# The one-token shift ahead of the FFN: two SBUF transfers in place of two matrix products, with the statistics later on VectorE

## The chip, the cores and the metric

The kernel runs on one core of a Trainium2 chip. The metric is device time in microseconds (us): the median of several executions. A profiled execution gives the trace that is read here, with its own span from the first to the last instruction.

The engines are TensorE (PE for its products, PEld for its weight loads), VectorE (DVE), ScalarE (ACT), GpSimd (POOL) and SyncE (SP). SP issues the transfers here. Each engine works through its own list in order, and engines wait for one another on semaphores.

## What is computed

A relative-position attention layer runs first, then six layers of local attention and a gated FFN. All of it is float32, over 4 sequences of 512 tokens of width 128. What matters for the change is the token shift: in each layer the second half of the features is taken from the token before.

```python
def shift_tokens(t):
    a, s = jnp.split(t, 2, -1)
    s = jnp.pad(s, ((0, 0), (1, 0), (0, 0)))[:, :-1]
    return jnp.concatenate([a, s], -1)

def ffn_layer(x, g, bln, W1, b1, W2, b2):
    mu = x.mean(-1, keepdims=True)
    var = ((x - mu) ** 2).mean(-1, keepdims=True)
    xn = (x - mu) / jnp.sqrt(var + 1e-05) * g + bln
    hg = xn @ W1 + b1
    a, gate = jnp.split(hg, 2, -1)
    return a * jax.nn.gelu(gate, approximate=False) @ W2 + b2

for i in range(DEPTH):
    x = attn_layer(shift_tokens(x), Wqkv[i], q_scale[i], k_scale[i], Wo[i]) + x
    x = ffn_layer(shift_tokens(x), ln_g[i], ln_b[i], W1[i], b1[i], W2[i], b2[i]) + x
```

## The kernel before

The six layers are `local_layers`. A tile is 128 tokens on the 128 partitions. A sequence is a group of SEQT = 4 tiles, a layer has 4 groups, and all six layers make NT = 96 tiles in GROUPS = 24 groups. The running activations stay in SBUF, in `x` (128 partitions, 16 tiles, 128 features).

Every engine runs one loop over periods n, one tile a period, and each function called in it names the tile it works on: `project("K", n)`, `turn_qk(0, n - 1)`, `attend(n - 3, 0)`. So the order on each engine is the order in which the loop's body is written. With step = n % 4 and g = n // 4, the FFN's work of a group is put at fixed steps. These are the places that matter:

- **PE, step 3** (`shift`, lines 545 to 554): between the two halves of `attend(n - 3)`, two products with the constant matrix `down` write the shifted half of the features of group g - 1 into the PSUM bank `XS`. The first moves rows 0 to 126 of each tile down by one, the second brings row 127 of a tile to row 0 of the next. Later in the same period come `turn_p` (line 510), `turn_xn` (line 561: transposes of the normalised tiles) and `project_out` (line 541).
- **DVE, step 3** (`statistics`, line 701): right after `rotate(1, n)` (line 643) DVE waits for the shift and takes mean and variance of the four tiles, from the own half in `x` and the shifted half in PSUM. Then come `sum_probs` (674), `invert`, `sum_squares` of q and of k (652), `offsets` (713) and `divide` (687), which `turn_p` of the same period waits for.
- **POOL, step 0 of the next group** (`deviations`, lines 281 and 283): the reciprocal deviation from the variances. It stands ahead of `norms` (from line 248) and `scale` (line 275) of the next tile, which end in the q that `turn_qk` (line 473) transposes on PE.
- **ACT, step 0 of the next group** (`normalise`, line 393): eight activations that make `xn` from `x` and the shifted half. PE's `turn_xn` waits for them.
- **SP** (`windows`, lines 180 to 189): for each tile t, 16 transfers of 64 KB that copy v into `vwin`, 32 partitions at a time. They wait for `v_copied` of tile t and, because `vwin` has two buffers, for `o_summed`: `attend(t - 2)` must be done. Weights of the next layer are loaded by SP at n % 16 == 10.

In the period 4g + 3 PE runs `attend(4g)`. Its end is what SP's `windows(4g + 2)` waits for.

Of the kernel before, what the change touches and what calls it, by code (L numbers as in the profile page):

```python
# [8 lines left out]
P = 128  # L9
# [23 lines left out]
MASKED = -1e30  # L33
FIRST_BITS = float(0x5f3759df)
NEWTON = 3
TABLES = 2 + 2 * 2 * WT + 5

def at_least(eng, sem, count):

    if count > 0:
        eng.wait_ge(sem, count)

def local_layers(nc, x1, x, out_tiles, w, kept):
# [7 lines left out]
    with ExitStack() as ctx:  # L53
        def sb(name, shape, dt=F32):
            return ctx.enter_context(nc.sbuf_tensor(name, shape, dt))
# [9 lines left out]
        b2 = sb("b2", [P, 2, D])  # L65
        qkscale = sb("qkscale", [P, 2, 2, DH])
        ropes = sb("ropes", [P, 2, 2, SEQT * 2, DH])
        ident, identb, bias, down, rope = (kept[n] for n in ("ident", "identb", "bias", "down", "rope"))

        first_stats = sb("first_stats", [P, TILES, 6])  # L70
        first_meanvar = sb("first_meanvar", [P, TILES, 2])
# [21 lines left out]
        meanvar = sb("meanvar", [P, SEQT, 2])  # L93
        rstd = sb("rstd", [P, SEQT])
        offset = sb("offset", [P, SEQT])
        xn = sb("xn", [P, SEQT, D])
        xnT = sb("xnT", [P, SEQ])
        gelu = sb("gelu", [FW, 2, SEQ])
# [9 lines left out]
                 "k_made k_squared k_rotated k_added k_summed k_roped k_turned kT_copied clamped newtoned rnorm_made "  # L108
                 "v_made v_copied scored maxed scores_taken exped p_turned p_copied p_summed rinv_made p_normed o_summed "
                 "oT_copied y_made y_added stats_made b2_added var_made var_eps rstd_made ropes_made "  # L110
                 "offset_made xn_made xn_turned xnT_copied shifted h_made gelu_made h_ready f_made x_done finished stored").split()
        s = {n: ctx.enter_context(nc.semaphore("l_" + n)) for n in names}
        placed, tail = (s["placed0"], s["placed1"]), (s["tail0"], s["tail1"])
        PLACED, TAIL, LOADS = 14 * 16, 2 * 16, 6 * 16
        CLEARED = 3

        ROOM = {"K": 0, "QT": 1, "XT": 4, "H0": 2, "H1": 1, "H2": 0, "O": 2, "XS": 3, "F": 3, "KT": 1, "V": 0, "S": 2, "Q": 1, "PT": 0, "XN": 3, "Y": 4}
        FREED = {"Q": ("q_squared",), "K": ("k_squared",), "V": ("v_copied",), "QT": ("qT_copied",),
                 "KT": ("kT_copied",), "S": ("scores_taken",), "PT": ("p_copied",), "O": ("oT_copied",),  # L120
                 "H": ("gelu_made", "h_ready"), "XT": ("xT_copied",), "XN": ("xnT_copied",), "XS": ("xn_made",), "Y": ("y_added",),
                 "F": ("x_done",)}

        ONE = ("XT", "XN", "XS", "Y", "F")

        def room(kind, c=0):
            return ROOM[kind + str(c)] if kind == "H" else ROOM[kind]
# [1 line left out]
        def bank(kind):  # L129

            r = room(kind)
            return ring[:, r, 0, :] if r < 3 else (tpose, yps)[r - 3][:, :]
# [11 lines left out]
        def halves_of(g, tile):  # L144

            half = D // 2
            return x[:, g % BATCH * SEQT + tile, 0:half], bank("XS")[:, tile * half:(tile + 1) * half]

        def live(t):
            return 0 <= t < NT  # L150
# [1 line left out]
        def lives(g):  # L152
            return 0 <= g < GROUPS
# [10 lines left out]
        @block.sync  # L164
        def _(sp):
            def load_layer(layer):
                p = layer % 2
                at_least(sp, s["x_done"], BATCH * (layer - 1))
                sp.dma_start(qkscale[:, p, :, :], w["qk"][layer]).then_inc(s["scales_in"], 16)
                sp.dma_start(wqkv[:, p, :], w["wqkv"][layer]).then_inc(s["qkv_in"], 16)  # L170
                loads = [(w1[:, p, :], w["w1"][layer]), (w2[:, p, :, :], w["w2"][layer]),
                         (b1[:, p, :], w["b1"][layer]), (ln[:, p, :], w["ln"][layer]), (b2[:, p, :], w["b2"][layer]),
                         (wo[:, p, :, :], w["wo"][layer])]
                for dst, src in loads:
                    sp.dma_start(dst, src).then_inc(s["weights"], 16)

            def windows(t):
                if live(t):
                    p = t % 2
                    sp.wait_ge(s["v_copied"], t + 1)  # L180
                    at_least(sp, s["o_summed"], t - 1)
                    for r in range(2):
                        sp.dma_start(vwin[W2 * r:W2 * r + W, p, 0, :], v[P - W:P, (t + 2) % 3, r, :]).then_inc(tail[p], 16)
                    for win in range(WT):
                        for r in range(2):
                            rows = v[W * win:W * win + W, t % 3, r, :]
                            sp.dma_start(vwin[W2 * r + W:W2 * r + W2, p, win, :], rows).then_inc(placed[p], 16)
                            if win + 1 < WT:
                                sp.dma_start(vwin[W2 * r:W2 * r + W, p, win + 1, :], rows).then_inc(placed[p], 16)

            load_layer(0)
            sp.wait_ge(s["cleared"], CLEARED)
            for n in range(NT):
                windows(n)
                if n % (SEQT * BATCH) == 10 and n // (SEQT * BATCH) + 1 < DEPTH:
                    load_layer(n // (SEQT * BATCH) + 1)
            for b in range(BATCH):
                sp.wait_ge(s["finished"], b + 1)
                tiles = slice(b * SEQT, (b + 1) * SEQT)
                sp.dma_start(out_tiles[:, tiles, :], x[:, tiles, :]).then_inc(s["stored"], 16)  # L200
            sp.wait_ge(s["stored"], 16 * BATCH)

        @block.gpsimd
        def _(pool):
            nc.gpsimd.memset(v[:, 2, :, :], 0.0).then_inc(s["cleared"], 1)
            nc.gpsimd.memset(kT[:, :, 0:W], 0.0).then_inc(s["cleared"], 1)
            nc.gpsimd.memset(power[:, :], -0.5).then_inc(s["ready"], 1)
            nc.gpsimd.memset(eps[:, :], EPS).then_inc(s["ready"], 1)
            pool.wait_ge(s["ready"], 2)
# [221 lines left out]
        def _(pe):  # L431
# [110 lines left out]
                                                stop=j == PAIRS - 1)  # L542
                    last.then_inc(s["y_made"], 1)

            def shift(g):

                if lives(g):
                    pe.wait_ge(s["y_added"], SEQT * (g + 1))
                    at, half = g % BATCH * SEQT, D // 2
                    out = take("XS", g)[:, 0:SEQT * half].rearrange("p (t d) -> p t d", d=half)  # L550
                    nc.tensor.matmul(out[:, :, :], down[:, 0, :], x[:, at:at + SEQT, half:D], start=True, stop=False,  # L551
                                     skip_group_check=True)
                    nc.tensor.matmul(out[:, 1:SEQT, :], down[:, 1, :], x[:, at:at + SEQT - 1, half:D], start=False, stop=True,
                                     skip_group_check=True).then_inc(s["shifted"], 1)

            def turn_xn(g):
                if lives(g):
                    pe.wait_ge(s["xn_made"], g + 1)
# [47 lines left out]
            for n in PERIODS:  # L606
                step, g = n % SEQT, n // SEQT
                project("K", n)
                turn_qk(0, n - 1)
                turn_x(n + 2)  # L610
                if step == 0:
                    hidden(g - 2, 0)
                    hidden(g - 2, 1)
                    hidden(g - 2, 2)
                attend(n - 3, 0)
                if step == 3:
                    shift(g - 1)
                if step == 1:
                    project_ffn(g - 2)
                turn_qk(1, n - 1)  # L620
                attend(n - 3, 1)
                project("V", n)
                scores(n - 1, 0)
                project("Q", n + 1)
                scores(n - 1, 1)
                turn_p(n - 2)
                if step == 3:
                    turn_xn(g - 1)
                project_out(n - 3)

        @block.vector
        def _(dve):
# [62 lines left out]

            def statistics(g):
                if lives(g):
                    dve.wait_ge(s["shifted"], g + 1)
                    for tile in range(SEQT):
                        for n, half in enumerate(halves_of(g, tile)):  # L700
                            nc.vector.bn_stats(stats[:, tile, n, :], half).then_inc(s["stats_made"], 1)  # L701
# [63 lines left out]
            for n in PERIODS:  # L765
# [5 lines left out]
                take_scores(n - 2)  # L771
                add_y(n - 4)
                rotate(1, n)
                if step == 3:
                    statistics(g - 1)
                sum_probs(n - 2)
                invert(n - 2)
                sum_squares(0, n)
                if step == 0:
                    gate(g - 2, 0)  # L780
                    gate(g - 2, 1)
                    gate(g - 2, 2)
# [6 lines left out]
            dve.wait_ge(s["x_done"], GROUPS)  # L789

def layer_tables(nc, pool, ident, identb, bias, down, made):

    nc.gpsimd.memset(down[:, :, :], 0.0).then_inc(made, 1)
    nc.gpsimd.memset(bias[:, :, :, :], 0.0).then_inc(made, 1)
    done = 2
    for first in range(2):
        for win in range(WT):
            view = bias[W * win:W * win + W, first, :, :]
# [10 lines left out]
        pool.wait_ge(made, done + r + 1)  # L810
    nc.gpsimd.tensor_copy(identb[:, :], ident[:, :]).then_inc(made, 1)

    nc.gpsimd.tensor_copy(down[:, 0, 1:P], ident[:, 0:P - 1]).then_inc(made, 1)
    nc.gpsimd.tensor_copy(down[:, 1, 0:1], ident[:, P - 1:P]).then_inc(made, 1)

def layer_norm_tiles(nc, src, dst, name):
# [33 lines left out]
def relative_attention(nc, x_in, x1, attn, w, scratch, kept, rope):  # L851
# [9 lines left out]
    with ExitStack() as ctx:  # L861
# [19 lines left out]
        with ExitStack() as second:  # L881
# [76 lines left out]
            with nc.Block() as block:  # L958
# [202 lines left out]
                def _(pool):  # L1161
# [1 line left out]
                    pool.wait_ge(s["filled"], 1)  # L1163
                    nc.gpsimd.memset(vaug[:, :, :, DP:DP + 1], 1.0).then_inc(s["cleared"], 1)
                    pool.wait_ge(loaded, LOADS)
                    layer_tables(nc, pool, ident, kept["identb"], kept["bias"], kept["down"], kept["made"])
                    for c in range(ROUNDS):
                        for k in range(2):
                            pool.wait_ge(s["c_taken"], 2 * c + k + 1)
# [53 lines left out]
def whole_kernel(nc, x_in, out, attention, layers):  # L1223
    with ExitStack() as ctx:
        def sb(name, shape, dt=F32):
# [4 lines left out]
        x_tiles = x_in.rearrange("b s d -> (b s) d").rearrange(tiled, p=P)  # L1230

        x = sb("x", [P, TILES, D])
        kept = {"ident": sb("ident", [P, P]), "identb": sb("identb", [P, P], BF16), "down": sb("down", [P, 2, P]),
                "bias": sb("bias", [P, 2, PAIRS, W2], BF16), "rope": sb("rope", [P, 2, SEQT * 2, DH]),
                "wo": sb("wo_a", [P, D]), "bo": sb("bo", [P, D])}
        for n in ("made", "rope_loaded", "x1_loaded", "x1_biased"):
# [94 lines left out]
```

## Time and profile before

| | before |
|---|---|
| median of 3 runs | 2145.36 us (2140.11 to 2148.38) |
| span of the profiled execution | 2143.9 us |
| PE busy | 2022.6 us (94%) |
| DVE busy | 1497.0 us (70%) |
| ACT busy | 1286.6 us (60%) |
| POOL busy | 1522.5 us (71%) |

The page lists the busy time of each engine, the granted TensorE clock in slices of the span, the chain of work that ended last, the costliest groups of instructions by line, and the transfers. The trace can also be asked for one engine's instructions in order of time. In that view a row starts with the start time and the duration in us, and a note in brackets tells how long the engine had sat idle and what ended that. A duration of "x2" is from the start of the first to the end of the second. For SP a row is the issue of transfers, marked SPq, and not the time the data moves. The layers run from about 485 us to the end.

### The profile page before, as it was taken

What the parts mean: (1) busy time and instruction counts of PE and PEld (TensorE: products, weight loads), DVE (VectorE), ACT (ScalarE), POOL (GpSimd) and SP (SyncE); (2) the same over time, 40 slices, a digit from 0 to 9 for tenths busy, and PEclk for the clock granted to TensorE, in tenths of its full rate; (3) what the DMA queues carried; (4) which work ended last, traced back from release to release, by engine and by line L of the source; (5) the groups of instructions that cost most, each with busy time, mean ns of one, the idle gap of its engine ahead of it and who ended that gap; (6) DMA issues with size and microseconds to landing.
All of it is one profiled execution on the core that took longest, in us unless ns stands there. A gap on an engine that the chain in (4) does not pass through costs nothing.

```text
span 2143.9 us, 84229 instructions
## 1 busy us (share of the span) xinstructions
PE 2022.6 (94%) x35763; PEld 1356.1 (63%) x35763; DVE 1497.0 (70%) x2268; ACT 1286.6 (60%) x1844; POOL 1522.5 (71%) x2307
## 2 busy tenths in 40 slices
PE   4789999878999999999999999999999999999997
PEld 1455555545666667666766667666676666766675
DVE  2445454458877887777877787777877788778773
ACT  3567777634656665665656565566656666566653
POOL 3344444458878887788877778778887788777880
PEclk8899999998999999999999999999999999999998
DMA  4999999932323222242222422224222242222221
GB/s 125 289 347 355 344 357 344 348 126 61 74 62 111 68 65 65 63 113 67 72 62 62 113 62 69 65 62 120 63 66 62 63 117 70 62 62 63 68 72 43
DMA packets 120004, 261.51 MB, mean 122 GB/s; under 512 B 29092, under 2 KB 34128, under 8 KB 118864
## 3 DMA queue, kind: packets, MB, share of 16 engines
q1 hardware_dynamic: 119632, 256.13, 41.4%
q8 instruction: 285, 4.67, 1.0%
q14 instruction: 87, 0.71, 0.1%
HBM read 87.06 MB, written 68.29 MB: 72 GB/s over the span
## 4 chain that ended last, share of the span: by engine, by line
PE 68%; POOL 4%; DVE 3%; issue 2%; ACT 1%; POOLq 0%; DVEq 0%; ACTq 0%
PE ring L463 22%; PE ring L529 9%; PE ring L473 8%; PE yps L541 7%; PE ring L499 7%; PE ring L569 5%; PE ring L510 4%; PE tpose L579 3%; PE ring L491 1%; POOL roped L275 1%; DVE turned L643 1%; PE tpose L551 1%; DVE ss L652 1%; DVE stats L701 0%; POOL ss L248 0%
## 5 line engine op out<-in xcount | busy, mean ns | idle before, releaser
L643 DVE TENSOR_TENSOR turned<-ring,ropes 128x1024 f32<-128x1024 f32 x384 | 452.0, 1219 | 303.0 <-PE ring L463 303.0
L240 POOL TENSOR_TENSOR roped<-turned 128x512 f32<-128x512 f32 x384 | 522.5, 1386 | 170.4 <-PE ring L473 169.0
L463 PE MATMUL ring<-wqkv,xT 128*128 128x512 f32 x1152 | 567.4, 616 | 5.2 <-ACT xT L328 4.0
L275 POOL TENSOR_TENSOR roped<-roped,rnorm 128x1024 f32<-128x1024 f32 x192 | 361.5, 1904 | 7.5
L1170 POOL TENSOR_SCALAR less<-less,lowest 128x512 f32<-128x512 f32 x256 | 175.3, 697 | 240.0 <-DVE lowest L1139 240.0
L1139 DVE CUSTOM_DVE_ANT_0 less<-ps_b,shifted 128x512 f32<-128x512 f32 x256 | 166.6, 688 | 226.0 <-PE ps_b L1002 79.7
L463 PEld LDWEIGHTS ring<-wqkv,xT 128*128 128x128 f32 x1152 | 198.2, 192 | 161.0 <-issue 149.8
L369 ACT COPY pT<-ring 128x1024 f32<-128x1024 f32 x96 | 97.2, 1012 | 305.8 <-PE ring L510 305.8
L529 PEld LDWEIGHTS ring<-pT,vwin 64*64 64x64 f32 x12288 | 198.5, 134 | 51.9 <-issue 51.5
L317 ACT ACTIVATE squares<-ring 128x1024 f32<-128x1024 f32 x192 | 197.3, 1028 | 55.8 <-DVE turned L643 55.8
L529 PE MATMUL ring<-pT,vwin 64*64 64x32 f32 x12288 | 219.7, 220 | 4.9 <-issue 3.4
L652 DVE TENSOR_REDUCE ss<-squares 128x16 f32<-128x1024 f32 x192 | 221.3, 1184 | 1.2 <-ACT squares L317 0.9
L473 PEld LDWEIGHTS ring<-ident,roped 128*128 128x128 f32 x1536 | 174.5, 142 | 70.0 <-issue 38.4
L473 PE MATMUL ring<-ident,roped 128*128 128x128 f32 x1536 | 204.4, 276 | 8.7 <-ACT qT L335 2.9
L499 PEld LDWEIGHTS ring<-kT,qT 64*32 64x32 f32 x12288 | 139.5, 105 | 100.8 <-issue 99.2
L1002 PE MATMUL ps_b<-posm,qvT 32*128 32x512 f32 x512 | 149.1, 666 | 52.3 <-DVE lowest L1139 43.6
L541 PE MATMUL yps<-wo,oT 128*128 128x128 f32 x1536 | 188.3, 276 | 1.2 <-ACT oT L376 1.1
L541 PEld LDWEIGHTS yps<-wo,oT 128*128 128x128 f32 x1536 | 180.0, 193 | 1.6 <-ACT oT L376 1.6
L499 PE MATMUL ring<-kT,qT 64*32 64x64 f32 x12288 | 173.0, 224 | 4.9 <-issue 4.9
L1068 PEld LDWEIGHTS ps_b<-ident,less 128*128 128x128 f32 x1024 | 111.5, 142 | 94.3 <-POOL less L1170 79.2
L344 ACT COPY kT<-ring 128x1024 f32<-128x1024 f32 x96 | 97.0, 1011 | 100.6 <-PE ring L473 100.6
L1213 ACT ACTIVATE pT_a<-ps_b 128x512 f32<-128x512 f32 x256 | 141.3, 613 | 25.3 <-PE ps_b L1068 25.2
(133 smaller groups left out, 3234.7 us busy)
## 6 DMA issues: line engine op xcount, KB each, us to landing
vwin<-v SPq DMA_DIRECT2D x1536, 64.0 KB, 2.0
shifted<-scratch_w SPq DMA_DIRECT2D x64, 1024.0 KB, 12.6
scratch_w<-wrows SPq DMA_DIRECT2D x48, 1026.0 KB, 10.9
scratch_w<-x SPq DMA_DIRECT2D x16, 1026.0 KB, 10.4
wqkv<-in_l_wqkv SPq DMA_DIRECT2D x6, 1536.0 KB, 6.9
wo<-in_l_wo SPq DMA_DIRECT2D x6, 512.0 KB
w<-in_l_w SPq DMA_DIRECT2D x6, 342.0 KB
w<-in_l_w SPq DMA_DIRECT2D x6, 171.0 KB
```

Of the source, the lines that this page charges most:

```text
L240: nc.gpsimd.tensor_tensor(halves[2][:, :, side, :], halves[0][:, :, side, :], halves[1][:, :, 1 - side, :], ALU.add).then_inc(s[name + "_a ...
L275: nc.gpsimd.tensor_tensor(whole, whole, norm, ALU.mult).then_inc(s[name + "_roped"], 1)
L317: nc.scalar.activation(squares[:, n, :], ring[:, room(name.upper()), :, :].rearrange("p b c -> p (b c)"), ACT.Square).then_inc(s[name + "_ ...
L463: last = nc.tensor.matmul(out[:, half, :], xT[:, t % SEQT * P:(t % SEQT + 1) * P], wqkv[:, layer_of(t), at + half * 512:at + (half + 1) * ...
L473: last = nc.tensor.transpose(out[:, j * P:(j + 1) * P], roped[:, n, j * P:(j + 1) * P], ident[:, :])
L499: last = nc.tensor.matmul(out[W * win:W * win + W, r, j * W2:(j + 1) * W2], qT[rows, j, W * win:W * win + W], kT[rows, j, at:at + W2], sta ...
L529: last = nc.tensor.matmul(out[a * DH:(a + 1) * DH, r, at:at + W], vwin[rows, p, win, j * DH:(j + 1) * DH], pT[rows, j, W * win:W * win + W ...
L541: last = nc.tensor.matmul(out[:, 0:D], oT[:, j % 2, j // 2, :], wo[:, layer_of(t), j, :], start=j == 0, stop=j == PAIRS - 1)
L643: ins = nc.vector.tensor_tensor(turned[:, n, part, :].rearrange("p (h d) -> p h d", d=DH), heads, table, ALU.mult)
L652: nc.vector.tensor_reduce(ss[:, n * HEADS:(n + 1) * HEADS], squares[:, n, :].rearrange("p (h d) -> p h d", d=DH), AX.X, ALU.add).then_inc( ...
L1139: nc.vector.tensor_tensor_reduce(less[:, c % 2, k, :], ps[:, 2 + k, :], shifted[:, c // 2 % NR, k, c % 2, :], -SCALE0, HIGHEST, ALU.add, A ...
L1170: nc.gpsimd.tensor_scalar(less[:, c % 2, k, :], less[:, c % 2, k, :], -1.0, lowest[:, c % 2, k:k + 1], ALU.mult, ALU.add).then_inc(s["scal ...
```

## The change

`shift` leaves PE and becomes two transfers on SP's queue for each group, into a new SBUF tile `behind`. The first takes 127 partitions, four tiles and 64 features: row p of `x` goes to row p + 1 of `behind`. The second takes row 127 of three tiles to row 0 of the tiles after them. Row 0 of the first tile is zeroed once by POOL. The matrix `down`, the bank `XS` and PE's two products are gone. On DVE `statistics` moves behind `sum_probs`, `invert` and `sum_squares(0, n)`, and waits for the transfers.

```diff
+            def shift(g):
+
+                at, half = g % BATCH * SEQT, D // 2
+                sp.wait_ge(s["y_added"], SEQT * (g + 1))
+                at_least(sp, s["xn_made"], g)
+                sp.dma_start(behind[1:P, :, :], x[0:P - 1, at:at + SEQT, half:D]).then_inc(s["behind_in"], 16)
+                sp.dma_start(behind[0:1, 1:SEQT, :], x[P - 1:P, at:at + SEQT - 1, half:D]).then_inc(s["behind_in"], 16)
+
             load_layer(0)
             sp.wait_ge(s["cleared"], CLEARED)
             for n in range(NT):
                 windows(n)
+                if n % SEQT == 2 and n >= SEQT:
+                    shift(n // SEQT - 1)
                 if n % (SEQT * BATCH) == 10 and n // (SEQT * BATCH) + 1 < DEPTH:
                     load_layer(n // (SEQT * BATCH) + 1)
+            shift(GROUPS - 1)
...
-            def shift(g):
-
-                if lives(g):
-                    pe.wait_ge(s["y_added"], SEQT * (g + 1))
-                    at, half = g % BATCH * SEQT, D // 2
-                    out = take("XS", g)[:, 0:SEQT * half].rearrange("p (t d) -> p t d", d=half)
-                    nc.tensor.matmul(out[:, :, :], down[:, 0, :], x[:, at:at + SEQT, half:D], start=True, stop=False,
-                                     skip_group_check=True)
-                    nc.tensor.matmul(out[:, 1:SEQT, :], down[:, 1, :], x[:, at:at + SEQT - 1, half:D], start=False, stop=True,
-                                     skip_group_check=True).then_inc(s["shifted"], 1)
...
                 attend(n - 3, 0)
-                if step == 3:
-                    shift(g - 1)
                 if step == 1:
                     project_ffn(g - 2)
...
             def statistics(g):
                 if lives(g):
-                    dve.wait_ge(s["shifted"], g + 1)
+                    dve.wait_ge(s["behind_in"], BEHIND * (g + 1))
...
                 rotate(1, n)
-                if step == 3:
-                    statistics(g - 1)
                 sum_probs(n - 2)
                 invert(n - 2)
                 sum_squares(0, n)
+                if step == 3:
+                    statistics(g - 1)
```

How this stands on the engines: on SP, at tile 10 (n = 4 x 2 + 2), the two transfers of group 1 come behind all 16 of `windows(10)`. A row is line, operation, tiles and shape, with the semaphores that it waits for. Lines are those of the changed kernel, six of the `windows` rows and those of the next layer's weights after it.

```order
L190 DMA vwin<-v 32x512
L188 DMA vwin<-v 32x512
L190 DMA vwin<-v 32x512
L188 DMA vwin<-v 32x512 x2
L197 DMA behind<-x 127x4x64 [waits l_xn_made,l_y_added]
L198 DMA behind<-x 1x3x64
L170 DMA qkscale<-in_l_qk 128x128
```

Before, the row of line 170's load followed the last `vwin` row directly, and SP had no part in the shift.

On DVE, period 4g + 3 from the second half of `rotate(1, n)` on, first before:

```order
L643 TENSOR_TENSOR turned<-ring,ropes 128x1024
L701 BN_STATS stats<-x 128x6 [waits l_shifted]
L701 BN_STATS stats<-tpose 128x6
L705 BN_AGGR meanvar<-stats 128x2 x3
L674 TENSOR_REDUCE rsum<-probs 128x16 [waits l_exped]
L681 RECIPROCAL rinv<-rsum 128x16 [waits l_p_summed]
L652 TENSOR_REDUCE ss<-squares 128x16 [waits l_rnorm_made,l_q_squared]
L652 TENSOR_REDUCE ss<-squares 128x16 [waits l_rnorm_made,l_k_squared]
L713 SCALAR_TENSOR_TENSOR offset<-meanvar,rstd 128x4 [waits l_rstd_made]
L687 TENSOR_TENSOR probs<-probs,rinv 128x1024 [waits l_rinv_made]
```

The same stretch of DVE in the changed kernel:

```order
L643 TENSOR_TENSOR turned<-ring,ropes 128x1024
L674 TENSOR_REDUCE rsum<-probs 128x16 [waits l_exped]
L681 RECIPROCAL rinv<-rsum 128x16 [waits l_p_summed]
L652 TENSOR_REDUCE ss<-squares 128x16 [waits l_rnorm_made,l_q_squared]
L701 BN_STATS stats<-x 128x6 [waits l_behind_in]
L701 BN_STATS stats<-behind 128x6
L705 BN_AGGR meanvar<-stats 128x2 x3
L652 TENSOR_REDUCE ss<-squares 128x16 [waits l_rnorm_made,l_k_squared]
L713 SCALAR_TENSOR_TENSOR offset<-meanvar,rstd 128x4 [waits l_rstd_made]
L687 TENSOR_TENSOR probs<-probs,rinv 128x1024 [waits l_rinv_made]
```

The statistics, here with two of their eight BN_STATS rows, moved behind three instructions of the attention's softmax and norms. The squares' sum of k, `offsets` and the division of the probabilities still stand behind them.

## Rows read from the trace of the kernel before

**Rows 1.** The page's head and its first section: busy us, share, instructions.

```profile
span 2143.9 us, 84229 instructions
PE 2022.6 (94%) x35763; PEld 1356.1 (63%) x35763; DVE 1497.0 (70%) x2268; ACT 1286.6 (60%) x1844; POOL 1522.5 (71%) x2307
```

**Rows 2.** The page's chain that ended last, shares by engine.

```profile
PE 68%; POOL 4%; DVE 3%; issue 2%; ACT 1%; POOLq 0%; DVEq 0%; ACTq 0%
```

**Rows 3.** PE in order of time, period 4g + 3: shift, attention's end, turn_p, next turn_qk.

```profile
1330.24 0.70 PE L551 MATMUL tpose<-x,down 128*128 128x256 f32 x2
...
1331.10 1.04 PE L473 MATMUL ring<-ident,roped 128*128 128x128 f32 x8
1332.07 1.13 PE L529 MATMUL ring<-pT,vwin 64*64 64x32 f32 x64
...
1338.88 1.09 PE L510 MATMUL ring<-ident,probs 128*128 128x128 f32 x8
...
1343.96 1.09 PE L473 MATMUL ring<-ident,roped 128*128 128x128 f32 x8
```

**Rows 4.** Line 551 alone: durations in ns (min/median/max), first and last start.

```profile
L551 PE MATMUL tpose<-x,down x48: 379/431/483, 578.8 to 2118.7; 128*128 128x256 f32 x48
```

**Rows 5.** DVE in order of time, the same period.

```profile
1327.64 0.28 DVE L694 TENSOR_TENSOR x<-yps,x 128x128 f32<-128x128 f32 x1
...
1331.30 0.23 DVE L701 BATCH_NORM_STATS2 stats<-x 128x6 f32<-128x64 f32 x1 [0.65 <-PE tpose L553]
...
1332.81 1.17 DVE L674 TENSOR_REDUCE rsum<-probs 128x16 f32<-128x1024 f32 x1
...
1334.18 2.28 DVE L652 TENSOR_REDUCE ss<-squares 128x16 f32<-128x1024 f32 x2
1336.38 0.15 DVE L713 SCALAR_TENSOR_TENSOR offset<-meanvar,rstd 128x4 f32<-128x4 f32 x1
```

**Rows 6.** SP's issues: first and last of windows(4g + 2), in two groups.

```profile
1265.92 1.14 SPq L183 DMA_DIRECT2D vwin<-v  x2
...
1275.27 1.22 SPq L187 DMA_DIRECT2D vwin<-v  x2
...
1333.31 1.80 SPq L183 DMA_DIRECT2D vwin<-v  x2
...
1343.95 1.23 SPq L187 DMA_DIRECT2D vwin<-v  x2
```

**Rows 7.** The page's transfers: tiles, queue, count, KB each, median us to landing.

```profile
vwin<-v SPq DMA_DIRECT2D x1536, 64.0 KB, 2.0
...
wqkv<-in_l_wqkv SPq DMA_DIRECT2D x6, 1536.0 KB, 6.9
...
w<-in_l_w SPq DMA_DIRECT2D x6, 171.0 KB
```

**Rows 8.** Windows: us, busy of PE, PEld, DVE, ACT, POOL, clock, DMA share, GB/s.

```profile
200.00:400.00 200.00, 182.24 (x2206) 111.22 (x2204) 97.29 (x307) 143.60 (x278) 91.53 (x134) 1.00 1.02 348
...
2142.10:2143.10 1.00, 0.00 (x0) 0.00 (x0) 0.00 (x0) 0.00 (x0) 0.00 (x0) 0.70 0.93 262
```

**Rows 9.** POOL in order of time: deviations, norms' first, both scales.

```profile
1334.74 0.20 POOL L281 TENSOR_TENSOR rstd<-meanvar,eps 128x4 f32<-128x4 f32 x1
...
1336.62 1.11 POOL L248 TENSOR_SCALAR ss<-ss 128x32 f32<-128x32 f32 x1 [0.58 <-DVE ss L652]
...
1342.00 3.77 POOL L275 TENSOR_TENSOR roped<-roped,rnorm 128x1024 f32<-128x1024 f32 x2
```

**Rows 10.** TensorE at either clock: PE rows, a window (columns as rows 8), statistics' first.

```profile
506.80 3.62 PE L463 MATMUL ring<-wqkv,xT 128*128 128x512 f32 x4
...
516.68 1.95 PE L463 MATMUL ring<-wqkv,xT 128*128 128x512 f32 x4 [1.19 <-ACT pT L369]
...
2121.80:2132.00 10.20, 5.68 (x10) 2.62 (x11) 0.24 (x2) 5.35 (x11) 1.88 (x2) 0.51 0.00 0
...
2119.44 0.23 DVE L701 BATCH_NORM_STATS2 stats<-x 128x6 f32<-128x64 f32 x1 [1.12 <-PE tpose L553]
...
2125.45 1.09 PE L561 MATMUL tpose<-ident,xn 128*128 128x128 f32 x4 [6.04 <-ACT xn L393]
```

More of the change, by code:

```diff
@@ L35 @@
 NEWTON = 3
-TABLES = 2 + 2 * 2 * WT + 5
+TABLES = 1 + 2 * 2 * WT + 3
 def at_least(eng, sem, count):
@@ L67, in local_layers @@
         ropes = sb("ropes", [P, 2, 2, SEQT * 2, DH])
-        ident, identb, bias, down, rope = (kept[n] for n in ("ident", "identb", "bias", "down", "rope"))
+        ident, identb, bias, rope = (kept[n] for n in ("ident", "identb", "bias", "rope"))
         first_stats = sb("first_stats", [P, TILES, 6])
@@ L95, in local_layers @@
         offset = sb("offset", [P, SEQT])
+        behind = sb("behind", [P, SEQT, D // 2])
         xn = sb("xn", [P, SEQT, D])
@@ L110, in local_layers @@
                  "oT_copied y_made y_added stats_made b2_added var_made var_eps rstd_made ropes_made "
-                 "offset_made xn_made xn_turned xnT_copied shifted h_made gelu_made h_ready f_made x_done finished stored").split()
+                 "offset_made xn_made xn_turned xnT_copied behind_in h_made gelu_made h_ready f_made x_done finished stored").split()
         s = {n: ctx.enter_context(nc.semaphore("l_" + n)) for n in names}
@@ L114, in local_layers @@
         PLACED, TAIL, LOADS = 14 * 16, 2 * 16, 6 * 16
-        CLEARED = 3
-        ROOM = {"K": 0, "QT": 1, "XT": 4, "H0": 2, "H1": 1, "H2": 0, "O": 2, "XS": 3, "F": 3, "KT": 1, "V": 0, "S": 2, "Q": 1, "PT": 0, "XN": 3, "Y": 4}
+        CLEARED, BEHIND = 4, 2 * 16
+        ROOM = {"K": 0, "QT": 1, "XT": 4, "H0": 2, "H1": 1, "H2": 0, "O": 2, "F": 3, "KT": 1, "V": 0, "S": 2, "Q": 1, "PT": 0, "XN": 3, "Y": 4}
         FREED = {"Q": ("q_squared",), "K": ("k_squared",), "V": ("v_copied",), "QT": ("qT_copied",),
                  "KT": ("kT_copied",), "S": ("scores_taken",), "PT": ("p_copied",), "O": ("oT_copied",),
-                 "H": ("gelu_made", "h_ready"), "XT": ("xT_copied",), "XN": ("xnT_copied",), "XS": ("xn_made",), "Y": ("y_added",),
+                 "H": ("gelu_made", "h_ready"), "XT": ("xT_copied",), "XN": ("xnT_copied",), "Y": ("y_added",),
                  "F": ("x_done",)}
-        ONE = ("XT", "XN", "XS", "Y", "F")
+        ONE = ("XT", "XN", "Y", "F")
         def room(kind, c=0):
@@ L146, in halves_of @@
             half = D // 2
-            return x[:, g % BATCH * SEQT + tile, 0:half], bank("XS")[:, tile * half:(tile + 1) * half]
+            return x[:, g % BATCH * SEQT + tile, 0:half], behind[:, tile, :]
         def live(t):
@@ L206, in _ @@
             nc.gpsimd.memset(kT[:, :, 0:W], 0.0).then_inc(s["cleared"], 1)
+            nc.gpsimd.memset(behind[0:1, 0, :], 0.0).then_inc(s["cleared"], 1)
             nc.gpsimd.memset(power[:, :], -0.5).then_inc(s["ready"], 1)
@@ L789, in _, with layer_tables @@
             dve.wait_ge(s["x_done"], GROUPS)
-def layer_tables(nc, pool, ident, identb, bias, down, made):
-    nc.gpsimd.memset(down[:, :, :], 0.0).then_inc(made, 1)
+def layer_tables(nc, pool, ident, identb, bias, made):
     nc.gpsimd.memset(bias[:, :, :, :], 0.0).then_inc(made, 1)
-    done = 2
+    done = 1
     for first in range(2):
@@ L811, in layer_tables @@
     nc.gpsimd.tensor_copy(identb[:, :], ident[:, :]).then_inc(made, 1)
-    nc.gpsimd.tensor_copy(down[:, 0, 1:P], ident[:, 0:P - 1]).then_inc(made, 1)
-    nc.gpsimd.tensor_copy(down[:, 1, 0:1], ident[:, P - 1:P]).then_inc(made, 1)
 def layer_norm_tiles(nc, src, dst, name):
@@ L1165, in _ @@
                     pool.wait_ge(loaded, LOADS)
-                    layer_tables(nc, pool, ident, kept["identb"], kept["bias"], kept["down"], kept["made"])
+                    layer_tables(nc, pool, ident, kept["identb"], kept["bias"], kept["made"])
                     for c in range(ROUNDS):
@@ L1232, in whole_kernel @@
         x = sb("x", [P, TILES, D])
-        kept = {"ident": sb("ident", [P, P]), "identb": sb("identb", [P, P], BF16), "down": sb("down", [P, 2, P]),
+        kept = {"ident": sb("ident", [P, P]), "identb": sb("identb", [P, P], BF16),
                 "bias": sb("bias", [P, 2, PAIRS, W2], BF16), "rope": sb("rope", [P, 2, SEQT * 2, DH]),
```

## The prediction, made before the changed kernel was run

> **What bounds the kernel now.** I read the page's head first. The profiled execution spans 2143.9 us, 1.5 us under the median of the runs (2145.36), so sums are made against 2143.9 and 1.5 is added at the end. PE is busy for 94% of the span [rows 1], and the chain that ended last runs 68% over PE [rows 2]. In the layers the next question is whether an engine makes PE wait, and where. So I took one period 4g + 3, the one with the shift, and read PE, DVE, SP and POOL in order of time.
>
> PE shows no idle note between its rows there [rows 3]. The shift occupies 1330.24 to 1331.10, which is 0.86 us, and it occurs 48 / 2 = 24 times [rows 4]. PE is the bound, but POOL is close behind. PE's next `turn_qk` of q stands at 1343.96, and POOL's first scale of that q ends at 1342.00 + 3.77 / 2 = 1343.89 [rows 3, 9]: PE is waiting for POOL at that one place.
>
> The view that decides is SP's. Its transfers of `windows(4g + 2)` begin at 1333.31, which is 0.11 after `attend(4g)` ends on PE (1332.07 + 1.13 = 1333.20), as the wait on `o_summed` demands [rows 3, 6]. They take SP from 1333.31 to 1343.95 + 1.23 = 1345.18, 11.9 us. In another group it is 1265.92 to 1276.49, 10.6 us. The mean is 11.2.
>
> **What goes from PE.** 24 times 0.86 us = 20.6 us at most. The removal of `down` and its preparation lies in the attention stage on POOL, is done once, and I cost it at nothing, since POOL has idle time there. The row 0 of `behind` costs one small memset, also nothing.
>
> **Where the transfers stand.** The change puts `shift(g - 1)` on SP behind `windows(4g + 2)`. DVE needs it in period 4g + 3: `add_y` ends at 1327.64 + 0.28 = 1327.92, then comes `rotate` of k. The statistics started at 1331.30 after 0.65 idle, so `rotate` ended at 1330.65. Now `sum_probs`, `invert` and one `sum_squares` stand ahead, 1332.81 to 1334.18 plus 1.10 (half of the pair's 2.28, overlap off) = 2.47 us [rows 5]. DVE reaches the new wait at 1333.12. The activations are ready at 1327.92, and the two places later buy 2.5 us. But SP first has 16 issues to make, which may not begin before `attend(4g)` is done. Without the 0.86 on PE that is at 1332.34, the first issue at 1332.45, the last one done at 1343.65. Only then are the shift's two transfers issued. **DVE waits for a transfer that is issued about 10.5 us after DVE got there**, whatever the transfer takes.
>
> **How long the transfer takes.** The trace of before has no transfer of this shape: 127 partitions in 508 pieces of 256 B. It is bounded from two sides.
>
> - The fixed part: a `vwin` transfer lands 2.0 us after its issue [rows 7]. Two 2 KB pieces an engine at 21.3 B/ns (348 GB/s over 16 engines at a share of 1.02 [rows 8]) are 0.2 of it, so 1.8 is fixed.
> - A piece: the last store moves 512 B pieces at 262 GB/s with a share of 0.93 [rows 8], so one engine makes 17.6 B/ns and a piece takes 29 ns. By its bytes at the rate of large pieces it would take 24, so 5 go with the piece itself. A 256 B piece is then 12 + 5 = 17 ns (estimate; ends 12 by bytes alone, 29 if a piece costs what the 512 B one does).
> - The number of engines. Evenly over 16: 32 pieces an engine, 0.5 us, landing after 2.4, and the second transfer, issued some 0.63 later, at about 2.5. On one engine: 508 x 17 ns = 8.6 us, landing after 10.4 (ends 7.9 and 16.5).
>
> The Trainium skill, "DMA: Bandwidth & Descriptors", section "Why a DMA increments its semaphore by 16 and not by 1", states that a transfer issued from SP uses the largest number of engines up to 16 that divides the slowest dimension on both sides, so 127 partitions go to a single engine. By that rule the sum below stands at about 2679; spread evenly it would be about 2490. The empty landing column for 114 partitions agrees, but no transfer of the kernel before shows 127.
>
> **What a late landing costs.** Let L be the landing: 1332.45 + 11.2 + 10.4 = 1354.05. From there the order on DVE is strict, and everything else waits for it.
>
> - POOL: the statistics take 1.5 (1331.30 to 1332.81 [rows 5]), deviations 1.3 (1334.74 to the end of the power, 1336.04), norms 5.4 (1336.62 to 1342.00), one scale 1.9 [rows 9]. With some 0.3 for semaphores, PE's `turn_qk` may start at L + 10.4.
> - PE: `offsets`, `normalise`, then `turn_xn`. The last group shows this run with nothing beside it: statistics at 2119.44, transposes at 2125.45, 6.0 us [rows 10]. After that come `project_out` and the K projection. From `turn_p` to `turn_qk`, 1338.88 to 1343.96, is 5.1 us, some 0.9 of it `turn_p` itself [rows 3], so at full clock PE would be there 4.2 after L + 6.0, at about L + 10.2. At full clock POOL and PE arrive together.
> - The clock: PE is without work from about 1338 to L + 4.6, when `turn_p` gets its divided probabilities: 21 us. In the last group 6.0 us without work took the granted clock to 0.51, and it stayed there to 2132.0, 6.5 us after PE resumed at 2125.45. At half clock the four rows of a projection take 3.62 in place of 1.95 [rows 10]. 6.5 us at half clock give 3.25 us of work. They cover `turn_p`, `turn_xn` and most of `project_out`, and K follows at full clock, at L + 12.7. I add 2.3 (ends 0, where POOL hides it, and 4.0, if all of it runs at half clock).
>
> So PE's `turn_qk` stands at L + 12.7 = 1366.75 in place of 1343.96: **22.8 us later in each group**, the 0.86 already in it. Nothing gives this back. Before, PE ran without idle from there to the next group's `attend(4g)`, so the next wait on SP is counted from the same place.
>
> There are 23 groups with windows on SP behind or ahead of their shift (0 to 22): 23 x 22.8 = 524 us. The last group's shift finds SP idle. `add_y` is done there some 1.1 us before 2119.44, and its statistics come 9.4 us later. Sum: 2143.9 + 524 + 9 + 1.5 = **2679 us**.
>
> Its own range: the piece from 12 to 29 ns moves each group by -2.5 to +6.2, the clock by -2.3 to +1.7, SP's issues by 0.6 either way. Not all together, that is 2590 to 2840.
>
> **The rivals.**
>
> - *Spread over 16 engines.* The same wait on SP's order, but the transfers land after 2.5 us, 7.9 sooner. 23 x 14.9 = 343, and 1.5 in the last group: **2490**. For it speaks that all loads timed in the profile move as if spread; against it the empty landing column. Chance 0.13.
> - *The transfer is out in time* (faster). If SP reaches the shift when `add_y` is done at 1327.92, and the transfer lands within 5.2 us (by 1333.12), DVE doesn't wait. PE saves 0.86, but POOL then waits for the statistics: var ready at 1334.7, deviations to 1336.0, norms at 1336.2 in place of 1336.62. PE's wait for POOL keeps half, and 0.43 x 24 = 10 us remain: **2135**. Against it speaks that SP's first issue follows `attend(4g)` by 0.11 in the trace. It decides when those 16 issues begin before 1322 or so. Chance 0.03.
> - *Out in time, but on one engine*: landing at 1338.4, PE 7.1 us late, 24 x 7 = 170: about 2316. Chance 0.03.
>
> **How the numbers follow.** One engine behind SP's queue 0.80, 16 engines 0.13, in time and fast 0.03, in time and slow 0.03, something else 0.01. The forecast is the first: 2679. Its own range holds about 0.7, so the range has to reach to the second: 2470 to 2840. A measurement of this kernel tells about 0.5% from no change. Faster by over 0.5% has 0.02, within 0.5% has 0.02 (the 2135 case lies at the border), slower 0.96.
>
> **What would show it.** Right: DVE idle before `stats` for about 21 us in each group, ended by a transfer of `behind`; the issue of `behind` on SP right behind 16 rows of `vwin`, some 11 us after `attend`; its landing about 10 us after that; PE idle before line 523 (`turn_p`) or so, with the granted clock down after it; a group's length of about 67 + 23 us (before, 2118.7 less 578.8 over 23 groups [rows 4]). An idle time of about 13 us with a landing of 2 to 3 us says 16 engines. Wrong would be a `behind` issue ahead of the `vwin` rows, a DVE that doesn't wait, or PE busy through 1338 to 1354 of this group.

## The result and the profile after

The changed kernel takes 2626.7 us (median of 4 runs, 2623.8 to 2632.8) against 2144.8 us for the kernel before. The ratio is 1.2246, with a 95% interval of 1.2206 to 1.2286. It is 482 us slower. The forecast was 2679 us, in a range of 2470 to 2840.

The page of the changed kernel has these lines in answer to [rows 1] and [rows 2]: busy us (share) and instructions, then the chain that ended last.

```profile
span 2622.0 us, 84082 instructions
PE 2046.9 (78%) x35667; PEld 1386.0 (53%) x35667; DVE 1500.9 (57%) x2268; ACT 1285.3 (49%) x1844; POOL 1515.2 (58%) x2305
...
PE 50%; SPq 10%; DMA 8%; DVE 6%; POOL 3%; issue 3%; ACT 2%; DVEq 0%; ACTq 0%; POOLq 0%
```

No engine's work grew by much. PE's busy time is up by 24 us although 96 instructions are gone, because part of it now runs at the lower clock (below). What is new is idle time. PE fell from 94% to 78%, and the chain now goes through SP's issues (10%) and the DMA of `behind` (8%), which had no share in it before.

Who waited for whom in the changed kernel: total us, times, longest.

```profile
DVE stats L701 <- DMA behind<-x: 467.8, 24, 21.1
...
PE ring L523 <- DVE probs L687: 443.4, 23, 21.7
```

DVE waits 24 times for the shift's transfers, 19.5 us each on average. PE waits 23 times for the divided probabilities that stand behind the statistics on DVE, 19.3 us each on average. Before, DVE's statistics waited 0.65 us in the group of [rows 5], and PE's `turn_p` stood there without an idle note [rows 3].

One group in order of time, SP first (issues), to be read against [rows 6]:

```profile
1197.19 1.47 SPq L184 DMA_DIRECT2D vwin<-v  x2
...
1206.79 1.23 SPq L188 DMA_DIRECT2D vwin<-v  x2
1208.11 0.76 SPq L197 DMA_DIRECT2D behind<-x  x1
1208.92 6.53 SPq L198 DMA_DIRECT2D behind<-x  x1
```

The same group on DVE, against [rows 5]:

```profile
1196.61 1.16 DVE L652 TENSOR_REDUCE ss<-squares 128x16 f32<-128x1024 f32 x1
1217.52 0.23 DVE L701 BATCH_NORM_STATS2 stats<-x 128x6 f32<-128x64 f32 x1 [19.74 <-DMA behind<-x]
```

And on PE, against [rows 3]:

```profile
1197.02 1.98 PE L476 MATMUL ring<-wqkv,xT 128*128 128x512 f32 x4
...
1221.89 1.97 PE L523 MATMUL ring<-ident,probs 128*128 128x128 f32 x8 [19.07 <-DVE probs L687]
1223.65 1.06 PE L563 MATMUL tpose<-ident,xn 128*128 128x128 f32 x4
1224.51 3.21 PE L554 MATMUL yps<-wo,oT 128*128 128x128 f32 x16
1227.56 1.88 PE L476 MATMUL ring<-wqkv,xT 128*128 128x512 f32 x4
1229.28 1.04 PE L486 MATMUL ring<-ident,roped 128*128 128x128 f32 x8
```

The three can be laid over each other. DVE is ready at 1197.8. SP begins its 16 `vwin` issues at 1197.19 and reaches the shift at 1208.11, 10.3 us after DVE. The data lands at 1217.5, 9.4 us after the issue. From there the chain is the forecast one: `turn_p` 4.4 later, `turn_xn` 6.1 later, the next `turn_qk` of q at 1229.28, 11.8 later. Over the 23 groups of this trace `turn_qk` comes 11.4 us after the statistics on average (10.3 to 12.1).

While the transfer runs, a window of this trace (us, busy of PE, PEld, DVE, ACT, POOL, then TensorE's clock, DMA share, GB/s) shows one DMA engine's worth of traffic:

```profile
1211.00:1216.00 5.00, 0.00 (x0) 0.00 (x0) 0.00 (x0) 0.00 (x0) 0.00 (x0) 0.50 0.08 18
```

18 GB/s is one piece of 256 B every 14 ns. A share of 0.08 of 16 engines is little more than one engine. No compute engine does anything in these 5 us, and TensorE's granted clock is 0.50, the lower of its two levels.

### The profile page after: what moved, and what is told of

Its sections match the earlier page's. It is cut to its first block, busy times and chain, and to the rows that moved or that the text cites. A ratio compares the mean times of both kernels' runs of the same rounds, so it can differ in the third digit from the quotient of the medians.

```text
span 2622.0 us, 84082 instructions
## 1 busy us (share of the span) xinstructions
PE 2046.9 (78%) x35667; PEld 1386.0 (53%) x35667; DVE 1500.9 (57%) x2268; ACT 1285.3 (49%) x1844; POOL 1515.2 (58%) x2305
## 4 chain that ended last, share of the span: by engine, by line
PE 50%; SPq 10%; DMA 8%; DVE 6%; POOL 3%; issue 3%; ACT 2%; DVEq 0%; ACTq 0%; POOLq 0%
PE ring L476 16%; DMA behind<-x 8%; PE ring L542 8%; PE yps L554 7%; PE ring L486 6%; SPq L188 5%; PE ring L523 4%; PE ring L512 4%; SPq L190 3%; PE tpose L581 3%; DVE turned L643 2%; DVE probs L687 1%; ACT L415 1%; SPq L184 1%; DVE stats L701 1%
## 5 line engine op out<-in xcount | busy, mean ns | idle before, releaser
L523 PE MATMUL ring<-ident,probs 128*128 128x128 f32 x768 | 125.0, 315 | 443.4 <-DVE probs L687 443.4
L523 PEld LDWEIGHTS ring<-ident,probs 128*128 128x128 f32 x768 | 98.6, 160 | 453.8 <-DVE probs L687 447.0
L701 DVE BATCH_NORM_STATS2 stats<-x 128x6 f32<-128x64 f32 x96 | 20.5, 214 | 467.8 <-DMA behind<-x 467.8
L406 ACT ACTIVATE xn<-x,offset,rstd 128x64 f32<-128x64 f32 x96 | 41.1, 428 | 495.5 <-DVE offset L713 495.5
L554 PE MATMUL yps<-wo,oT 128*128 128x128 f32 x1536 | 210.0, 296 | 1.9 <-ACT oT L389 1.1
L554 PEld LDWEIGHTS yps<-wo,oT 128*128 128x128 f32 x1536 | 204.0, 214 | 2.3 <-ACT oT L389 1.6
```

The lines of the kernel that those rows point to most:

```text
L523: last = nc.tensor.transpose(out[:, j * P:(j + 1) * P], probs[:, t % 2, j, :, :].rearrange("p r k -> p (r k)"), ident[:, :])
L554: last = nc.tensor.matmul(out[:, 0:D], oT[:, j % 2, j // 2, :], wo[:, layer_of(t), j, :], start=j == 0, stop=j == PAIRS - 1)
```

## The experiments

Times are given against the kernel before on the same chip, as ratios with their interval. The runs were made on several chips, on which the kernel before takes 2143.7 to 2159.3 us.

**The place on SP's queue.** e1_early puts the transfers ahead of `windows(4g + 2)`.

```diff
             for n in range(NT):
-                windows(n)
                 if n % SEQT == 2 and n >= SEQT:
                     shift(n // SEQT - 1)
+                windows(n)
```

> The changed kernel with one edit: on SP the shift's transfers stand ahead of windows(4g + 2) and not behind it. The transfer itself stays as it is. Theory (SP's order costs some 10.5 us a group, the one-engine transfer of 9.4 us the rest): the transfers are issued when add_y is done, which in the trace of before is 5.2 us ahead of the place where DVE needs them, so DVE waits about 4 us a group in place of 20. PE is then late by 4 us (POOL's chain of 10.4 us from the landing), by up to 5 if the clock falls: 24 x 4 to 5 on 2145, so 2240 to 2270 us. Rival (the transfer's length alone makes the loss, its place in SP's order little): the landing after the issue is the same, so the time stays above 2550. Rival (the place is all, the length little): 2130 to 2150.

Measured: 2299.7 us, 1.0726 (1.0702 to 1.0749). The place alone is worth 327 us, and both rivals are out. It missed the stated 2240 to 2270 by 30 us. The wait is 137.5 / 24 = 5.7 us a group, not 4. SP's issues in one group of e1:

```profile
1095.20 1.23 SPq L188 DMA_DIRECT2D vwin<-v  x2
1096.52 0.76 SPq L197 DMA_DIRECT2D behind<-x  x1
1097.32 6.53 SPq L198 DMA_DIRECT2D behind<-x  x1
```

DVE in the same group:

```profile
1095.04 0.28 DVE L694 TENSOR_TENSOR x<-yps,x 128x128 f32<-128x128 f32 x1
...
1105.92 0.23 DVE L701 BATCH_NORM_STATS2 stats<-x 128x6 f32<-128x64 f32 x1 [5.38 <-DMA behind<-x]
```

And the total of this wait in e1:

```profile
DVE stats L701 <- DMA behind<-x: 137.5, 24, 9.4
```

`add_y` ends at 1095.32, but SP is still at the last of `windows(4g + 1)` until 1096.43. The expectation had taken SP to be free at `add_y`. Over the first 23 groups the issue comes 1.45 us after `add_y`, and 23 x 1.45 = 33 us is most of the miss. The clock, for which the expectation had allowed up to 1 us a group, took 1.2: PE idles about 5 us here and comes back slower (a granted clock of 0.50 from 1110 to 1114 in the group shown), and `turn_qk` comes 11.5 us after the statistics on average, while POOL's scale is ready after 10.3.

**The number of DMA engines.** e2_spread cuts the 127 partitions into 112 and 15 and leaves the place. e8_prime cuts them into 113 and 14.

```diff
-                sp.dma_start(behind[1:P, :, :], x[0:P - 1, at:at + SEQT, half:D]).then_inc(s["behind_in"], 16)
+                for lo, hi in ((0, 112), (112, P - 1)):
+                    sp.dma_start(behind[lo + 1:hi + 1, :, :], x[lo:hi, at:at + SEQT, half:D]).then_inc(s["behind_in"], 16)
```

> The changed kernel with one edit: the transfer of 127 partitions is cut into one of 112 (16 x 7) and one of 15 partitions, at the same place behind windows(4g + 2). Theory: the 508 pieces no longer go through one DMA engine. Three transfers issued some 0.8 us apart, the last landing 2.0 after its issue, make about 3.5 in place of 9.4 us, 5.9 x 23 = 136 less: 2480 to 2495 us. DVE still waits some 14 us a group. Rival (the 9.4 us are a price of 256 B pieces between partitions, however they are cut): no change, about 2627, or slower by one more issue of 0.8 us a group.

Measured for e2: 2480.1 us, 1.1566 (1.1541 to 1.1591), 147 us under the changed kernel, as the theory had it.

> e2_spread with the cut one partition further: 113 and 14 partitions in place of 112 and 15. As many transfers and bytes; 113 is a prime, 112 is 16 x 7. Theory (equal shares decide how many DMA engines a transfer gets): the 113 go through one engine, 452 pieces of 14 ns, landing some 8.5 us after the issue in place of 3.5: 2590 to 2610 us. Rival (what counted in e2 is the cut in two): 2480, as e2.

Measured for e8, in two runs: 1.2176 (1.2110 to 1.2242), which is 2612 us on the scale of the other chip's 2144.8, a little above the theory's 2590 to 2610 and far from e2. SP's issues in a group of e2:

```profile
1249.57 1.65 SPq L198 DMA_DIRECT2D behind<-x  x2
1251.27 0.75 SPq L199 DMA_DIRECT2D behind<-x  x1
```

The start of the statistics on DVE there:

```profile
1253.03 0.23 DVE L702 BATCH_NORM_STATS2 stats<-x 128x6 f32<-128x64 f32 x1 [13.71 <-DMA behind<-x]
```

SP's issues in a group of e8:

```profile
1219.66 6.49 SPq L198 DMA_DIRECT2D behind<-x  x2
1226.20 0.73 SPq L199 DMA_DIRECT2D behind<-x  x1
```

The start of the statistics on DVE there:

```profile
1228.39 0.23 DVE L702 BATCH_NORM_STATS2 stats<-x 128x6 f32<-128x64 f32 x1 [19.26 <-DMA behind<-x]
```

From the first issue to the statistics it is 3.5 us with 112 and 15 partitions, and 8.7 us with 113 and 14. The bytes, the pieces and the number of transfers are the same. One partition decides. This is the rule that the prediction named from the Trainium skill, "DMA: Bandwidth & Descriptors", section "Why a DMA increments its semaphore by 16 and not by 1": the largest count of engines up to 16 that divides the slowest dimension. 112 is 16 x 7, while 113 and 127 are primes. The traces agree with it in all three cases.

**Both together.** e3_early_spread has both edits.

> Both edits together: the transfers ahead of windows(4g + 2), cut into 112 and 15 partitions. Theory: they land about 3.7 us after add_y, 1.5 us before DVE needs them. No wait is left on DVE, PE has lost its 0.86 us of products, and half of that is kept since POOL's chain ends 0.43 earlier a group: 2135 us, 0.5% under before. Rival (a shift by transfers costs something of its own, in later window transfers or in reads from SBUF): 2145 or more.

Measured: 2143.1 us, 1.0000 (0.9986 to 1.0014). The whole loss is gone. The two edits alone, 327 and 147, add up to nearly the 484 that both give. But the expected gain of 0.5% did not come. In a group of e3, SP's issues are:

```profile
1332.02 1.22 SPq L188 DMA_DIRECT2D vwin<-v  x2
1333.34 1.66 SPq L198 DMA_DIRECT2D behind<-x  x2
1335.04 0.75 SPq L199 DMA_DIRECT2D behind<-x  x1
```

DVE's `add_y` and the start of the statistics in that group:

```profile
1331.66 0.28 DVE L695 TENSOR_TENSOR x<-yps,x 128x128 f32<-128x128 f32 x1
...
1337.31 0.23 DVE L702 BATCH_NORM_STATS2 stats<-x 128x6 f32<-128x64 f32 x1
```

DVE's wait for the transfers over the whole of e3 (total us, times, longest):

```profile
DVE stats L702 <- DMA behind<-x: 13.1, 15, 3.5
```

The transfers are issued at 1333.34, 1.4 us after `add_y` (1331.94), because SP is still at the earlier windows. They land about when DVE needs them, and in 15 groups after that (13.1 us in all, 3.5 of it in the last group, where SP is free and the wait is the transfers' own time).

**Earlier still.** e6_between takes the cut of e2 and issues them between the 14th and the 15th transfer of `windows(4g + 1)`. e10_between_again is the same kernel on another chip.

```diff
-            def windows(t):
+            def windows(t, shifted=None):
...
                     for win in range(WT):
+                        if win == WT - 1 and shifted is not None:
+                            shift(shifted)
                         for r in range(2):
...
-                windows(n)
-                if n % SEQT == 2 and n >= SEQT:
-                    shift(n // SEQT - 1)
+                windows(n, n // SEQT - 1 if n % SEQT == 1 and n >= SEQT else None)
```

> e3_early_spread with the shift's transfers still earlier: on SP between the 14th and the 15th transfer of windows(4g + 1), and not behind all 16. Theory: in e3 they were issued 1.5 us after add_y, since SP was still at windows(4g + 1), DVE waited 0.39 us a group for them and this took away the gain. Without that wait DVE's statistics start 5.15 us after add_y, PE's turn_qk follows 10.3 later, 15.5 in place of 16.0 in the kernel before: 0.5 x 24 = 12 us, 2131 us. Rival (POOL or DVE hold PE elsewhere in the group, the products' 0.86 us were never on the path): 2140 to 2146.

Measured for e6: 2148.4 us, 0.9947 (0.9925 to 0.9969).

> e6_between once more, the same kernel. Theory: 0.995 of before (12 to 14 us less). Rival (its lead was the spread of that chip's runs): 1.0.

Measured for e10: 2133.4 us, 0.9937 (0.9915 to 0.9959). On both chips this kernel is faster than the kernel before, by 0.5 to 0.6%. SP in a group of e10:

```profile
1313.25 1.66 SPq L200 DMA_DIRECT2D behind<-x  x2
1314.95 0.75 SPq L201 DMA_DIRECT2D behind<-x  x1
1315.74 1.24 SPq L190 DMA_DIRECT2D vwin<-v  x2
1317.86 1.14 SPq L184 DMA_DIRECT2D vwin<-v  x2
```

DVE in the same group:

```profile
1312.94 0.28 DVE L695 TENSOR_TENSOR x<-yps,x 128x128 f32<-128x128 f32 x1
...
1317.28 1.16 DVE L653 TENSOR_REDUCE ss<-squares 128x16 f32<-128x1024 f32 x1
1318.36 0.21 DVE L702 BATCH_NORM_STATS2 stats<-x 128x6 f32<-128x64 f32 x1
```

`add_y` ends at 1313.22, the issue follows at 1313.25, and the statistics begin at 1318.36 with no idle note. The last two `vwin` issues still end at 1316.98, ahead of the next windows at 1317.86, so nothing is pushed back on SP in this group.

**The statistics' place.** e4_stats_late is the kernel before with the statistics moved and the products left on PE. e7_between_first is e6 with the statistics back ahead of `sum_probs`.

```diff
                 rotate(1, n)
-                if step == 3:
-                    statistics(g - 1)
                 sum_probs(n - 2)
                 invert(n - 2)
                 sum_squares(0, n)
+                if step == 3:
+                    statistics(g - 1)
```

> The kernel before with the second part of the change alone: the products stay on PE, the statistics move behind sum_probs, invert and sum_squares of q. Theory: harmless, since DVE loses its 0.65 us wait on PE and POOL's norms start 0.2 to 0.4 us earlier: 2138 to 2145 us. Rival (the later statistics hold POOL's deviations, and with it the norms and PE's next turn_qk): 0.5 to 1 us a group, 2157 to 2169 us.

Measured for e4: 2145.6 us, 1.0011 (0.9996 to 1.0025). Alone, this part of the change does nothing that can be measured, and the rival's 2157 to 2169 is out.

> e6_between with the statistics back at their place ahead of sum_probs. Theory: DVE is there 2.7 us after add_y, the transfers land at about 3.9, so DVE waits 1.2 us with three instructions behind it, and POOL's norms start 0.4 us later than in the kernel before: 2145 to 2157 us, which tells what the two places later are worth. Rival (the wait fits into DVE's idle time): as e6.

Measured for e7: 1.0112 (1.0074 to 1.0149), worse than expected. Against e6 on the same chip it is 1.7%, some 1.5 us a group. DVE in one group of e7:

```profile
1349.88 0.28 DVE L695 TENSOR_TENSOR x<-yps,x 128x128 f32<-128x128 f32 x1
1350.53 2.36 DVE L644 TENSOR_TENSOR turned<-ring,ropes 128x1024 f32<-128x1024 f32 x2 [0.38 <-PE ring L477]
1354.88 0.23 DVE L702 BATCH_NORM_STATS2 stats<-x 128x6 f32<-128x64 f32 x1 [1.99 <-DMA behind<-x]
```

And its wait in total:

```profile
DVE stats L702 <- DMA behind<-x: 37.3, 24, 3.5
```

The transfers land 3.5 to 5.0 us after `add_y`, DVE is there after 2.7, and the softmax's sum and the norms stand behind the wait. Ahead of the last group the wait is (37.3 - 3.5) / 23 = 1.5 us on average, where 1.2 was expected. So the later place is worth nothing while the shift is made on PE, and 1.7% once it comes by transfer.

**The clock.** e5_busy and e9_busy_longer are the changed kernel with extra products on PE, 18 and 21 a group, that are meant to fill its idle time ahead of `turn_p`.

```diff
+            def keep_busy(g):
+                if 0 <= g < GROUPS - 1:
+                    out = take("W", g)
+                    for _ in range(18):
+                        nc.tensor.matmul(out[:, :], ident[:, :], wqkv[:, layer_of(SEQT * g), 0:512], start=True, stop=True)
...
+                if step == 3:
+                    keep_busy(g - 1)
                 turn_p(n - 2)
```

> The changed kernel, and in each of the 23 groups with a wait PE makes 18 further products of 128x512 into the FFN's bank ahead of turn_p (some 17 us at full clock, inside its idle time of 19.3; what they write is overwritten by turn_xn). Theory (the granted clock falls in the idle time and holds project_out and the K projection back until 11.4 us after the landing, where POOL's chain alone would have let turn_qk start at 10.4): with PE at work the clock stays high, and 1.0 x 23 = 23 us go, 2604 us. Rival (the clock is hidden behind POOL, the 11.4 is POOL's own): 2627, no change.

Measured: 1.2252 (1.2201 to 1.2303), no change. The theory seemed to fall, but the trace showed that the edit had not done its work. PE still idled 3.7 us ahead of `turn_p` in the group shown (4.0 on average), and then ran `project_out` in 2.97 us, mostly at the lower clock. PE in a group of e5:

```profile
1235.20 1.09 PE L523 MATMUL ring<-ident,probs 128*128 128x128 f32 x8 [3.67 <-DVE probs L695]
1236.87 1.12 PE L569 MATMUL tpose<-ident,xn 128*128 128x128 f32 x4 [0.58 <-ACT xn L406]
1237.78 2.97 PE L554 MATMUL yps<-wo,oT 128*128 128x128 f32 x16
```

A window of that stretch of e5 (columns as above, the clock is third from the end):

```profile
1236.00:1240.00 4.00, 3.42 (x18) 3.18 (x17) 3.76 (x4) 3.58 (x7) 3.18 (x11) 0.57 0.00 0
```

> e5_busy with 21 further products in place of 18, so that PE's idle time ahead of turn_p falls from 4.0 to about 1.4 us a group. In e5 the granted clock still fell to 0.5 for one stretch just as PE resumed, and project_out took 2.97 us in place of 1.95. Theory (the clock holds turn_qk back by 0.9 us a group): with so little idle time the clock stays at 1.0, turn_qk starts 10.4 after the landing and the time is 0.9 x 23 = 21 us under the changed kernel's: 1.215 of before. Rival (turn_qk waits for something else after the landing): 1.2246 of before, as the changed kernel.

Measured: 2602.8 us, 1.2126 (1.2094 to 1.2158). That is 26 us (1.0%) under the changed kernel's ratio, and the two intervals leave 15 to 37. PE in a group of e9:

```profile
1222.34 1.10 PE L523 MATMUL ring<-ident,probs 128*128 128x128 f32 x8 [0.63 <-DVE probs L695]
1224.01 0.66 PE L569 MATMUL tpose<-ident,xn 128*128 128x128 f32 x4 [0.58 <-ACT xn L406]
1224.51 1.95 PE L554 MATMUL yps<-wo,oT 128*128 128x128 f32 x16
...
1228.26 1.09 PE L486 MATMUL ring<-ident,roped 128*128 128x128 f32 x8
```

The start of the statistics on DVE in that group:

```profile
1217.96 0.23 DVE L709 BATCH_NORM_STATS2 stats<-x 128x6 f32<-128x64 f32 x1 [19.69 <-DMA behind<-x]
```

A window of 400 us in e9:

```profile
1100.00:1500.00 400.00, 388.49 (x5879) 242.10 (x5877) 236.94 (x297) 184.65 (x243) 242.12 (x369) 1.00 0.23 57
```

The same window of the changed kernel:

```profile
1100.00:1500.00 400.00, 301.49 (x5621) 210.92 (x5604) 235.49 (x295) 183.15 (x241) 241.20 (x367) 0.87 0.23 57
```

With the clock at 1.00, `turn_qk` starts 10.3 us after the statistics (1217.96 to 1228.26), where POOL's chain lets it. In the changed kernel's group above it was 11.8. In 18 of e9's 23 groups it is 10.3, in the other five it is still 11.5 to 11.7.

## Why the prediction was right, and where its sizes were off

The mechanism came out step by step.

- **The place on SP** was read from the code and the issue's 0.11 us behind `attend`. Forecast: the issue 10.5 us after DVE's arrival. Measured: 10.3 in the group shown, 10.6 on average. e1 shows that it carries 327 of the 482 us.
- **One DMA engine** was chosen against 16 with 0.80. e2 and e8 show it. The step that rested on the empty landing column and on divisors held. The column by itself could not tell one engine from several: it is empty for `behind` in the changed kernel and in e2 alike.
- **The piece** was put at 17 ns with ends of 12 and 29, and measured 14. The landing took 9.4 us in place of 10.4, so each group is 1.0 us shorter, 24 us in all. The mis-sized part is the fixed 5 ns that a piece was given on top of its bytes, from the 512 B pieces of the last store. 508 x 3 ns would be 1.5 us. Some 0.5 came back, since the rest of the landing, 9.4 less 508 x 14 ns, is 2.3 us and not 1.8.
- **From the landing to `turn_qk`**, 10.4 us by POOL's rows, measured 10.3 in e9, where nothing else is in the way.
- **The clock** was put at 2.3 us a group from the last group of before. e9 makes it 26 / 23 = 1.1, and the changed kernel's trace says the same: `turn_qk` comes 11.4 us after the statistics on average, 1.1 behind the 10.3 of POOL's chain. In the row that was used, PE ran 6.5 us at half clock after its idle time. In the group shown, `turn_p` and the transposes ran at half clock and `project_out` in part (3.21 in place of 1.95 us), and K was back at 1.88. What `turn_p` lost cost almost nothing, which the sum had not seen: the transposes start 6.1 us after the statistics there and in e9 alike, where PE waits 0.58 us for `xn`. The clock's term is the larger error, 1.2 x 23 = 28 us.
- Together 24 + 28 = 52 us, which is the distance from 2679 to 2627. The traces agree without it: from `add_y` to `turn_qk` of q it is 36.6 us on average in place of 16.0 before, 20.5 us more in each of 23 groups, where the forecast had 22.8.

A wrong turn that the forecast did not pay for: its 2135 us case needs SP to be free when `add_y` is done, and the transfers of e1 and e3 were put where that was taken for granted. [rows 6] do not show the windows before these. In the trace of before they end at 1329.48, 1.6 us after `add_y` (1327.92):

```profile
1327.76 1.72 SPq L187 DMA_DIRECT2D vwin<-v  x2
```

In e3 the issue comes 1.5 us after `add_y` on average, and only the place between two `vwin` transfers gave the 0.5% that had been reckoned.

That the products on PE cost something is now shown too. e4 and e6 both have the later statistics and differ in how the shift is made. Without the products, with the transfers in time, the kernel is 0.5 to 0.6% faster, and e4 is not. That is less than their 20.6 us (1.0%), since POOL's chain then sets `turn_qk`: in e4 it comes 10.8 us after the statistics on average with POOL's scale ready after 10.3, in e10 10.3 with POOL's scale ready after 10.2. The gain lies in the layers and not in the attention stage, which lost the preparation of `down`: from the first group's `add_y` to the end of the trace it is 1567.5 us before, 1567.6 in e4, 1565.7 in e3, 1558.7 in e6 and 1555.7 in e10.

## What to carry to other kernels

A transfer put on a queue starts when the queue gets there: list what stands ahead of it on that queue and what those entries wait for, before asking how long it takes. Cut the partitions of a transfer so that their count shares out over the DMA engines; 112 and 15 landed in 3.5 us, 127 in one piece took 9.4. When both faults are cured and the expected gain still does not come, look where the queue stood when the data became ready: here 1.5 us of lateness on SP took the gain away.

## What the runs showed of the hardware that was not expected

- A transfer on one DMA engine also holds the queue that issues behind it. The issue of the shift's second transfer, three pieces, took SP 6.5 us in the changed kernel and 0.75 in e2. In e8 SP was held as well (6.49 us for two issues).
- A short idle time was enough to bring TensorE's granted clock down: in e5 some 4 us without work, after 16 us of products, left 0.57 over the next 4 us, and `turn_qk` came 11.2 us after the statistics on average, in e1 after 5 us without work 11.5. After the 19 us of idle time in the changed kernel it was 11.4. With the idle time at 0.63 us in the group shown of e9, the clock stayed at 1.00.
